# Six places for block rows, keys beside the gather, and output turns inside the last head

## The chip, the cores and the metric

The kernel runs on one core of a Trainium2 chip. A core has five engines that run their own instruction streams and meet at semaphores: PE (TensorE, matrix products and transposes), DVE (VectorE), ACT (ScalarE), POOL (GpSimd) and SP (SyncE, which here only issues DMAs). The metric is device time in microseconds of one execution, lower is better. About 0.2% (5 us) is what a measurement of this kernel can tell from no change.

## The reference

Four gated layers work on x, 2 batches of 1024 tokens with 256 channels, that is 2048 rows or 16 tiles of 128 tokens. All is fp32. Each layer adds an attention part and a feed-forward part to x, both times a tanh gate. The change touches the first three of these eight parts:

```
x = x + tanh(g_xattn[0]) * joint_attention(layernorm(x), context)   # 16 heads of 16; keys of x and of 154 context rows
x = x + tanh(g_ffn[0])   * one_expert(layernorm(x))                 # argmax of 8 experts, gelu, 256 -> 256 -> 256
x = x + tanh(g_xattn[1]) * cross_attention(layernorm(x), context)   # 16 heads of 64; keys and values of the context only
```

In the expert part each token goes through the one expert of eight that its gate ranks highest. In the cross-attention part keys and values are products of the context and of weights; neither depends on x. The queries come from a second layer norm of x with gain and shift.

## The kernel before

Products are made in three passes: each fp32 operand is split into an upper part (rounded to the PE's fp32r form by ACT) and a rest (made by DVE or POOL by a subtraction), and three matmuls add upper by upper, rest by upper and upper by rest. The helper `rest` is line 210, `three` is line 1640, `products` is line 198. The parts of the program follow one another in blocks; at the end of a block all engines meet, and `net.reclaim()` between the stages also clears semaphores.

**Joint attention** (`joint_attention`) runs 32 turns, one for each head of each batch. In a turn PE makes transposed scores for ten key tiles (line 2923), ACT takes exponentials of them (line 2986, two of 128x512 for each key tile), and PE multiplies them with the values (line 2933). Beside it DVE finds row maxima for a head that comes later; in the last turn none is left to find. A turned output is copied by ACT into `o_raw` (lines 2968 and 2976). The first batch's output is normalised by POOL during a later head. Then an output block follows: DVE normalises the second batch (lines 3157 and 3162), PE turns the 16 tiles (line 3100), ACT and DVE split them (lines 3132 and 210), PE multiplies them with `wo`, and DVE adds the products to x (line 3148) and takes row statistics for the next layer norm (lines 95 and 98).

**One expert** (`one_expert`) ranks the experts, gives each token a slot so that every block of 256 slots has one expert, and scatters the normalised rows to `slots_x` in HBM. The loop runs over 15 blocks. For block i, SP loads 256 rows (line 537) into one of NX = 3 places, PE turns them (line 560), ACT and DVE split them (lines 643 and 210), PE makes the hidden layer (`up(i)`, 12 matmuls of 256 columns), ACT applies gelu (line 667), DVE splits it (lines 205 and 210), PE makes the output (`down_mm(i)`, again 12), DVE copies it (line 723) and SP stores it to `slots_y` (line 549). The weights of block i+2 are copied by ACT (line 636) after `down_mm(i-1)`, and their rest is made by POOL (line 210). PE's order is `up(i+1)`, turn of block i+3, `down_mm(i)`. SP's order is load of block i+3, wait for the copied output of block i, store of block i. After the loop POOL waits for the stores and fetches the rows of each token back by 16 indirect DMAs (line 696); DVE adds them to x in four groups and takes statistics (lines 779, 95, 98).

**Cross attention** (`cross_attention`) first runs the layer norm with gain and shift into `xT`, then a block that makes keys and values (ACT splits upper parts, DVE and POOL make rests, PE multiplies; DVE copies values), and then the main block, whose first product needs the split of the first group of rows (`xg`).

Of the kernel before, what the change touches and what calls it, by code (L numbers as in the profile page):

```python
# [19 lines left out]
F32R = mybir.dt.float32r  # L20
ALU = mybir.AluOpType
# [3 lines left out]
P = 128  # L25
# [5 lines left out]
G = 4  # L31
# [5 lines left out]
BLOCK = 256  # L37
NB0 = (NTOK + 8 * (BLOCK - 1)) // BLOCK
# [447 lines left out]
def one_expert(net, xT, xn, x, w, const, scale, slots_x, slots_y, cleared, fetch):  # L486
# [8 lines left out]
    NX, NW, NH, NY = 3, 3, 3, 3  # L495
# [3 lines left out]
    with ExitStack() as ctx:  # L499
# [9 lines left out]
        place, slot, slots = sb("place", [P, T, E]), sb("slot", [P, T]), sb("slots", [P, T], mybir.dt.uint32)  # L509
# [4 lines left out]
        yg = xn  # L514
# [10 lines left out]
        gathered = [sem(f"gathered{g}") for g in range(G)]  # L525
        x_in = [sem(f"x_in{k}") for k in range(NX)]
        stored = [sem(f"stored{k}") for k in range(NY)]
        order = [(n % G) * GT + n // G for n in range(T)]
# [4 lines left out]
        def _(sp):  # L533
# [11 lines left out]
            for i in range(NB):  # L545
                if i + NX < NB:
                    load(i + NX)
                sp.wait_ge(y_taken, i + 1)
                sp.dma_start(rows(slots_y, i), yb[:, i % NY].rearrange("p (h d) -> p h d", h=H))\
                    .then_inc(stored[i % NY], 16)  # L550

        @block.tensor
        def _(pe):
# [10 lines left out]
            def up(i):  # L564
# [4 lines left out]
                for u in range(2):  # L569
                    for c in range(C):  # L570
                        ins = products(pe, net.ps[:, GATE + i % 2, u * BLOCK:(u + 1) * BLOCK],
                                       lambda a: w_parts[a][:, i % NW, 512 * u + c * P:512 * u + (c + 1) * P],
                                       lambda a: x_parts[a][:, i % NX, c * BLOCK:(c + 1) * BLOCK],
# [55 lines left out]
        def _(act):  # L629
# [9 lines left out]
            def take_x(i):  # L639
                act.wait_ge(turned, i + 1)  # L640
                if i >= NX:
                    act.wait_ge(up_done, i - NX + 1)
                act.copy(x_parts[0][:, i % NX, :].bitcast(F32R), net.ps[:, XB[i % len(XB)], :]).then_inc(x_upper, 1)
# [29 lines left out]
            net.rows.root_table(act)  # L673

        @block.gpsimd
        def _(pool):
# [3 lines left out]
            for n, t in enumerate(order):  # L680
# [11 lines left out]
            for k in range(NY):  # L692
                pool.wait_ge(stored[k], 16 * len(range(k, NB, NY)))
            for n in sorted(range(T), key=lambda n: order[n]):
                t = order[n]
                pool.indirect_dma_start(yg[:, t, :], None, slots_y, bass.IndirectOffsetOnAxis(slots[:, n:n + 1], 0))\
                    .then_inc(gathered[t // GT], 16)

        @block.vector
        def _(v):  # L700
# [6 lines left out]
            def rest_x(i):  # L707
                v.wait_ge(x_upper, i + 1)
                rest(v, x_parts[1][:, i % NX, :], net.ps[:, XB[i % len(XB)], :], x_parts[0][:, i % NX, :])\
# [64 lines left out]
            v.wait_ge(init_taken, 2 * G)  # L774
            for g in range(G):
                v.wait_ge(gathered[g], 16 * GT)
                for t in range(g * GT, (g + 1) * GT, 2):
                    xk, yk = (ap[:, t:t + 2, :].rearrange("p t d -> p (t d)") for ap in (x, yg))
                    step(v.scalar_tensor_tensor(xk, yk, scale, xk, ALU.mult, ALU.add))
                step.settle()  # L780
                net.rows.take(v, step, x, range(g * GT, (g + 1) * GT))
# [863 lines left out]
def cross_attention(net, x, factor, w):  # L1645
# [5 lines left out]
    with ExitStack() as outer:  # L1651
# [10 lines left out]
        with ExitStack() as ctx:  # L1662
            layer_norm(net, x, xT, again=True, gain=w("gain"), shift=w("shift"), after=w)
# [7 lines left out]
            wq_upper, wo_upper, cleared, x_upper = sem("wq_upper"), sem("wo_upper"), sem("cleared"), sem("x_upper")  # L1671
# [31 lines left out]
            def _(act):  # L1703
                act.copy(cx[0][:].bitcast(F32R), net.ctxT).then_inc(ctx_upper, 1)
# [6 lines left out]
                act.copy(wq[0][:].bitcast(F32R), w("wq")).then_inc(wq_upper, 1)  # L1711
# [3 lines left out]
                act.copy(wo[0][:].bitcast(F32R), w("wo")).then_inc(wo_upper, 1)  # L1715

            @block.gpsimd
            def _(pool):
                for part in ct:
                    ins = pool.memset(part[:], 0.0)  # L1720
                ins.then_inc(cleared, 1)
# [1856 lines left out]
```

## Time and profile before

| | |
|---|---|
| median of 3 runs | 2550.1 us (2546.55 to 2551.69) |
| the profiled execution | 2544.47 us, of which the span is 2541.5 us |
| mean granted PE clock | 0.901 of full |
| busy: PE, DVE, ACT, POOL | 2058.8, 1769.8, 1328.3, 1049.7 us |

The span runs from the first to the last instruction. Busy time is a sum over the whole span, over stages with different limits. The three places of the change lie between 488 us and 745 us of the span: the last head's turn and the output block (488 to 533), the expert loop (577 to 674), the gather (674 to 703), the layer norm (704 to 714), the keys and values (714 to 739), and the first products of the main block (from 740).

### The profile page before, as it was taken

Reading aid. Unit: us, or ns where it says so; the run is one execution under the profiler, and the core shown is the slowest. Engines: PE = TensorE matmul, PEld = TensorE weight load, DVE = VectorE, ACT = ScalarE, POOL = GpSimd, SP = SyncE. Lnnn points to the kernel's source line nnn. Section 1 sums busy time; section 2 is a strip of 40 time slices with the busy share of each in tenths; the row PEclk is TensorE's granted clock in tenths of the full one; section 3 lists DMA queues with packets and bytes.
Section 4 is the critical chain, followed back from the end, with each engine's and each line's share of the span. In section 5 each row is a group of like instructions: output and inputs, shape, how many; then the busy total and the mean of one; then the engine's idle time right before and its main releaser. Section 6 shows DMA issues by size and latency. Waiting matters only on the chain. (4 is left out here: it accounts for less than half of the span.)

```text
span 2541.5 us, 41197 instructions
## 1 busy us (share of the span) xinstructions
PE 2058.8 (81%) x14707; PEld 1493.9 (59%) x14744; DVE 1769.8 (70%) x3781; ACT 1328.3 (52%) x3055; POOL 1049.7 (41%) x1062
## 2 busy tenths in 40 slices
PE   6899999955479998699998978976998886985254
PEld 5344444345366665588887667765877765764122
DVE  6899999654465555577776676666657676568896
ACT  4588888823255553333333246464435565323797
POOL 1333333023444442255553655552636462422554
PEclk9899999978789998799999898988998988997586
DMA  4244444152200000300001000002000000001000
GB/s 108 32 54 54 50 54 50 19 228 81 83 1 1 1 1 1 129 1 1 1 1 63 23 1 1 1 1 93 1 1 1 1 1 38 1 4 55 0 1 33
DMA packets 27719, 80.79 MB, mean 32 GB/s; under 512 B 6016, under 2 KB 18048, under 8 KB 25856
## 3 DMA queue, kind: packets, MB, share of 16 engines
q0 software_dynamic: 9600, 22.38, 6.8%
q1 hardware_dynamic: 17920, 55.80, 6.4%
q8 instruction: 120, 1.97, 0.3%
q14 instruction: 79, 0.65, 0.1%
HBM read 45.07 MB, written 12.06 MB: 22 GB/s over the span
## 5 line engine op out<-in xcount | busy, mean ns | idle before, releaser
L2986 ACT ACTIVATE probs<-psum 128x512 f32<-128x512 f32 (+1 forms) x640 | 343.9, 601 | 91.3 <-PE psum L2923 75.9
L3025 DVE TENSOR_REDUCE max_parts<-psum 128x1 f32<-128x512 f32 x512 | 320.0, 685 | 26.9 <-PE psum L2871 21.2
L198 PE MATMUL psum<-x_upper,weights_upper 128*128 128x512 f32 (+2 forms) x556 | 221.5, 398 | 26.0 <-POOL weights_rest L210 12.9
L210 POOL TENSOR_TENSOR weights_rest<-L1f,weights_upper 128x256 fp32r<-128x256 f32 x216 | 178.8, 855 | 148.8 <-ACT weights_upper L340 148.8
L2923 PE MATMUL psum<-q_stack,k_stack 50*128 50x512 f32 (+1 forms) x640 | 235.9, 453 | 0.3 <-ACT probs L2986 0.3
L198 PE MATMUL psum<-x_rest,weights_upper 128*128 128x512 f32 (+2 forms) x556 | 218.4, 393 | 0.0
L198 PE MATMUL psum<-x_upper,weights_rest 128*128 128x512 f32 (+2 forms) x556 | 217.0, 390 | 0.0
L2871 PE MATMUL psum<-k_stack,q_stack 48*128 48x512 f32 x512 | 192.8, 465 | 12.8 <-ACT probs L2986 7.7
L2933 PE MATMUL psum<-probs,v_tok 128*17 128x256 f32 x2560 | 195.3, 387 | 0.2 <-ACT probs L2986 0.2
L198 PE MATMUL psum<-weights_upper,hidden_upper 128*128 128x256 f32 (+1 forms) x572 | 180.3, 315 | 5.4 <-DVE hidden_rest L210 2.7
L2516 POOL TENSOR_TENSOR probs<-probs,row_sum 128x1024 f32<-128x1024 f32 x64 | 121.2, 1896 | 138.6 <-DVE row_sum L2535 138.6
L210 POOL TENSOR_TENSOR weights_rest<-L2f,weights_upper 128x256 fp32r<-128x256 f32 (+1 forms) x144 | 104.5, 754 | 163.4 <-ACT weights_upper L340 163.4
L198 PE MATMUL psum<-weights_upper,hidden_rest 128*128 128x256 f32 (+1 forms) x572 | 165.1, 289 | 0.0
L198 PE MATMUL psum<-weights_rest,hidden_upper 128*128 128x256 f32 (+1 forms) x572 | 165.0, 289 | 0.0
L2871 PEld LDWEIGHTS psum<-k_stack,q_stack 48*128 48x128 f32 x512 | 80.0, 189 | 125.0 <-DVE max_parts L3025 69.2
L2484 ACT ACTIVATE probs<-probs,row_least 128x256 f32<-128x256 f32 x256 | 127.0, 498 | 40.6 <-DVE row_least L2529 40.6
L2643 POOL DMA_DIRECT2D q_stack<-q_parts x56 | 30.5, 544 | 264.4 <-PE psum L2923 264.4
L210 DVE TENSOR_TENSOR hidden_rest<-hidden,hidden_upper 128x512 fp32r<-128x512 f32 (+1 forms) x143 | 132.8, 929 | 4.9
L198 PEld LDWEIGHTS psum<-x_upper,weights_upper 128*128 128x128 f32 (+1 forms) x556 | 107.0, 193 | 49.5 <-issue 22.1
L1927 ACT ACTIVATE L1x<-psum,row_least 128x154 f32<-128x154 f32 x256 | 95.6, 400 | 76.3 <-DVE row_least L1981 76.3
L1963 POOL TENSOR_TENSOR L1x<-L1x,row_sum 128x512 f32<-128x512 f32 x64 | 67.8, 1059 | 157.7 <-DVE row_sum L1986 157.3
L2381 POOL TENSOR_TENSOR cos_part<-cos_part,sin_part 128x1024 f32<-128x1024 f32 x32 | 76.5, 2389 | 115.6 <-DVE sin_part L2348 115.6
(508 smaller groups left out, 6061.0 us busy)
## 6 DMA issues: line engine op xcount, KB each, us to landing
k_stack<-k_parts POOLq DMA_DIRECT2D x56, 147.2 KB, 3.8
L1f<-in_L1f SPq DMA_DIRECT2D x1, 6016.0 KB, 22.4
L2f<-in_L2f SPq DMA_DIRECT2D x2, 2268.0 KB, 8.6
L1x<-in_L1x SPq DMA_DIRECT2D x1, 4226.0 KB, 14.6
k_stack<-k_parts POOLq DMA_DIRECT2D x56, 73.6 KB, 4.1
L0f<-in_L0f SPq DMA_DIRECT2D x1, 4096.0 KB, 13.7
L2a<-in_L2a SPq DMA_DIRECT2D x2, 2048.0 KB, 14.7
slots_x<-zeros SPq DMA_DIRECT2D x1, 3840.0 KB, 12.8
```

The costliest lines, as they stand in the source:

```text
L198: ins = pe.matmul(out, lhsT(a).bitcast(F32R), rhs(b).bitcast(F32R), start=start and n == 0, stop=stop and n == len(PASSES) - 1, skip_group ...
L210: return engine.tensor_tensor(dst.bitcast(F32R), src, up_part, ALU.subtract)
L1927: ins = act.activation(ex[:, n % NE, h, :], net.ps[:, SLOT + 2 * s + e, a * SC:(a + 1) * SC], ACT.Exp, bias=mn[:, s, e, a:a + 1], scale=-1 ...
L1963: pool.tensor_tensor(main, ex[:, n % NE, :, 0:P], spread(sm[:, n % NE, :], P), ALU.mult)
L2381: pool.tensor_tensor(cp, cp, s_part[:, t % NSP].rearrange("p a n -> p (a n)"), ALU.add).then_inc(added, 1)
L2484: ins = act.activation(pb[:, n % NPB, h, :], pb[:, n % NPB, h, :], ACT.Exp, bias=mn[:, n % NPB, h:h + 1], scale=-1.0, accum_out=sm[:, n % ...
L2516: pool.tensor_tensor(pb[:, n % NPB], pb[:, n % NPB], spread(sm[:, n % NPB, :], 2 * P), ALU.mult)\
L2871: ins = pe.matmul(out, qs[s][r, a * P:(a + 1) * P].bitcast(F32R), ks[s][r, k * 512:(k + 1) * 512].bitcast(F32R), start=True, stop=True)
L2923: pe.matmul(net.ps[0:m, ST + n % NS, :], ks[s][r, k * P:k * P + m].bitcast(F32R), qs[s][r, :].bitcast(F32R), start=True, stop=True).then_i ...
L2933: ins = pe.matmul(net.ps[32 * j:32 * j + HD + 1, PVB, 0:256], vt[:, b, k, h, :], pb[:, n % NPB, j * 256:(j + 1) * 256], start=k == 0, stop ...
L2986: act.activation(pb[0:m, n % NPB, (1 - e) * 512:(2 - e) * 512], net.ps[0:m, ST + (2 * n + e) % NS, :], ACT.Exp, scale=HD ** -0.5)\
L3025: ins = v.tensor_reduce(mx3[:, u % 2, a + 4 * e, k:k + 1], src, AX.X, ALU.max)
```

## The change

It has three parts.

First, the rows of a block get six places in SBUF (`NX = 6`) where they had three; the split rows keep three (`NP = 3`). SP issues six loads at the start, and in the loop the load of block i+6 stands where that of block i+3 stood.

Second, the gather of the expert part moves into the keys block of cross attention, and the layer norm moves behind that block. The gathered rows go into the memory of `xT`. What POOL did there goes elsewhere: tails of the context are copied by ACT, `ct` and `vz` are cleared by DVE, the second half of `wv` and all of `wo` get their rest from DVE. DVE adds the gathered rows group by group after each pair of value items. The split of the first row group moves to the start of the main block, upper by ACT and rest by DVE, and PE waits for it. The table load for the square root moves from the end of the expert loop to the end of ACT's queue in the keys block.

Third, six of the eight output turns of joint attention (four tiles each) are made in the last head's turn, together with their splits and that of `wo`, in memory of `k_parts`. The two that are left need the last eight heads of the second batch.

```diff
-    NX, NW, NH, NY = 3, 3, 3, 3
+    NX, NP, NW, NH, NY = 6, 3, 3, 3, 3
...
-        x_parts, w_parts = two("x", [P, NX, C * BLOCK]), two("weights", [P, NW, 4 * BLOCK])
+        x_parts, w_parts = two("x", [P, NP, C * BLOCK]), two("weights", [P, NW, 4 * BLOCK])
...
@@ one_expert, sync @@
+            for k in range(NY):
+                sp.wait_ge(stored[k], 16 * len(range(k, NB, NY)))
...
@@ one_expert, end of the gpsimd queue @@
-            for k in range(NY):
-                pool.wait_ge(stored[k], 16 * len(range(k, NB, NY)))
-            for n in sorted(range(T), key=lambda n: order[n]):
-                t = order[n]
-                pool.indirect_dma_start(yg[:, t, :], None, slots_y, bass.IndirectOffsetOnAxis(slots[:, n:n + 1], 0))\
-                    .then_inc(gathered[t // GT], 16)
...
@@ cross_attention, keys block, scalar @@
+                act.wait_ge(tails_cleared, 1)
+                act.wait_ge(ctx_upper, 1)
+                tails(ct[0], cx[0])
+                act.wait_ge(ctx_ready, 1)
+                tails(ct[1], cx[1]).then_inc(tails_ready, 1)
...
                 act.copy(wo[0][:].bitcast(F32R), w("wo")).then_inc(wo_upper, 1)
+                act.copy(wq[0][:].bitcast(F32R), w("wq")).then_inc(wq_upper, 1)
+                net.rows.root_table(act)
...
@@ keys block, gpsimd @@
+                for n in sorted(range(T), key=lambda n: SLOT_TILE[n]):
+                    t = SLOT_TILE[n]
+                    pool.indirect_dma_start(yg[:, t, :], None, slots_y, bass.IndirectOffsetOnAxis(slots[:, n:n + 1], 0))\
+                        .then_inc(gathered[t // GT], 16)
                 pool.wait_ge(wq_upper, 1)
                 rest(pool, wq[1][:], w("wq"), wq[0][:])
-                pool.wait_ge(wo_upper, 1)
-                rest(pool, wo[1][:], w("wo"), wo[0][:])
+                pool.tensor_scalar(gbo[:], w("bo"), factor, None, ALU.mult)
...
@@ keys block, vector @@
+                for n in range(len(v_items)):
+                    value(n)
+                    if n == 1:
+                        v.wait_ge(wo_upper, 1)
+                        rest(v, wo[1][:], w("wo"), wo[0][:])
+                    if n % 2:
+                        add(n // 2)
...
+        layer_norm(net, x, xT, again=True, gain=w("gain"), shift=w("shift"))
...
@@ main block: scalar, vector, tensor @@
+                act.copy(xg[0][:, 0].bitcast(F32R), whole_x(0)).then_inc(first_upper, 1)
+                v.wait_ge(first_upper, 1)
+                rest(v, xg[1][:, 0], whole_x(0), xg[0][:, 0]).then_inc(first_ready, 1)
+                pe.wait_ge(first_ready, 1)
...
@@ joint_attention @@
+            turns = [(0, 0), (0, 1), (1, 0), (1, 1), (2, 0), (3, 0)]
+            turn_at = {0: [0], 1: [1], 2: [2], 3: [3], 4: [4, 5]}
...
+                        if u == NU - 1:
+                            for i in turn_at[k]:
+                                turn_o(i)
...
+                        if u == NU - 1 and k == 0:
+                            act.copy(wo[0][:].bitcast(F32R), w_out("wo")).then_inc(wo_upper, 1)
+                        if u == NU - 1 and k % 2 == 0 and k > 0:
+                            for i in turn_at[k // 2 - 1]:
+                                upper_o(i)
...
+                for i in turn_at[STEPS - 1]:
+                    upper_o(i)
                 copy_out(NU - 1)
                 take_out(NU - 1)
...
@@ output block, tensor @@
+                for g in range(LATE):
+                    project(g)
+                for g in range(LATE, G):
+                    pe.wait_ge(normed, g - LATE + 1)
+                    for j in range(GT):
+                        t = g * GT + j
+                        ins = pe.transpose(net.ps[:, TB + g - LATE, j * P:(j + 1) * P],
+                                           qp[0][:, 1, t // QT, t % QT * P:(t % QT + 1) * P], net.ident[:])
+                    ins.then_inc(turned, 1)
+                for g in range(LATE, G):
+                    project(g)
```

ACT's queue at the last head, before. `probs` are the exponentials, `o_heads` and `o_raw` a head's finished output, `oT_upper` the upper parts of the turned outputs.

```order
L2986 ACTIVATE probs<-psum 128x512 x6
L2976 COPY o_raw<-psum 128x4x17 x2
L2986 ACTIVATE probs<-psum 128x512 x8
L2986 ACTIVATE probs<-psum 26x512 x2
L2968 COPY o_heads<-psum 128x256
L2976 COPY o_raw<-psum 128x4x17 x2
L2797 UNCONDITIONAL_BRANCH
L3126 UNCONDITIONAL_BRANCH
L3128 CAST wo_upper<-L0o 128x512
L3132 CAST oT_upper<-psum 128x512 x8
```

The same end of ACT's queue after the change. `k_parts` is the memory in which the split turns now stand.

```order
L3018 CAST k_parts<-psum 128x512
L3032 ACTIVATE probs<-psum 128x512 x4
L3018 CAST k_parts<-psum 128x512
L3032 ACTIVATE probs<-psum 128x512 x2
L3032 ACTIVATE probs<-psum 26x512 x2
L3018 CAST k_parts<-psum 128x512 x2
L3004 COPY o_heads<-psum 128x256
L3012 COPY o_raw<-psum 128x4x17 x2
L2811 UNCONDITIONAL_BRANCH
L3181 UNCONDITIONAL_BRANCH
L3186 CAST k_parts<-psum 128x512 x2
```

Six of the eight casts of turned outputs moved from the output block to between the exponentials, two of them to just before the last head's copy.

POOL's queue from the gather on, before. `xn` and, after the change, `xT` take the gathered rows; the `ISA` row is the clearing of semaphores between stages.

```order
L696 DMA xn<-slots_y,slots 128x256 x16
L499 UNCONDITIONAL_BRANCH
L79 ISA x2
L1717 UNCONDITIONAL_BRANCH
L1720 MEMSET context_tails_upper 128x512
L1720 MEMSET context_tails_rest 128x512
L1726 CAST context_tails_upper<-context_upper 128x8x26 x2
L1726 CAST context_tails_rest<-context_rest 128x8x26 x2
L1730 MEMSET tail_values 128x2048
L210 TENSOR_TENSOR wv_rest<-L1x,wv_upper 128x2x512
L1734 TENSOR_SCALAR gated_bias<-L1x,cross_factor 128x256
L210 TENSOR_TENSOR wq_rest<-L1x,wq_upper 128x2048
```

POOL's queue at the same place after.

```order
L500 UNCONDITIONAL_BRANCH
L80 ISA x3
L1717 UNCONDITIONAL_BRANCH
L1721 DMA xT<-slots_y,slots 128x256 x16
L211 TENSOR_TENSOR wq_rest<-L1x,wq_upper 128x2048
L1725 TENSOR_SCALAR gated_bias<-L1x,cross_factor 128x256
```

The 16 gathers stand inside the keys block, and all that POOL computed there but one rest and the bias is gone from its queue.

DVE's queue in the keys block after the change (the adds of groups 2 and 3 follow in the same way).

```order
L211 TENSOR_TENSOR wv_rest<-L1x,wv_upper 128x2x512 x2
L1766 MEMSET tail_values 128x2048
L211 TENSOR_TENSOR keys_rest<-psum,keys_upper 128x308 x8
L1736 COPY values<-psum 128x512 x2
L211 TENSOR_TENSOR wo_rest<-L1x,wo_upper 128x2048
L1749 SCALAR_TENSOR_TENSOR x_tok<-xT,tanh_gates,x_tok 128x512 x2
L96 BN_STATS row_stats<-x_tok 128x6 x4
L99 BN_AGGR mean_var<-row_stats 128x2 x4
L1741 COPY tail_values<-psum 32x2x64 x8
L1749 SCALAR_TENSOR_TENSOR x_tok<-xT,tanh_gates,x_tok 128x512 x2
```

The adds and statistics, which stood alone after the loop, now stand between the copies of values.

## Rows read from the trace of the kernel before

**Rows 1.** Busy time by stretch: us, PE, PEld, DVE, ACT, POOL busy; clock, DMA, GB/s.

```profile
488.00:506.00 18.00, 17.51 (x169) 6.36 (x167) 0.56 (x2) 16.37 (x36) 0.00 (x0) 1.00 0.01 1
577.00:674.00 97.00, 62.24 (x420) 58.75 (x420) 46.61 (x60) 37.39 (x61) 29.69 (x28) 0.88 0.25 79
```

**Rows 2.** Waits in the expert loop, 578 to 674: us in total, times, longest.

```profile
PE psum L560 <- DMA block_x<-slots_x: 45.5, 12, 17.5
```

**Rows 3.** Timeline of SP's queue: start us, us, queue, line, out<-in.

```profile
591.44 0.36 SPq L549 DMA_DIRECT2D slots_y<-block_y  x1
591.84 0.47 SPq L537 DMA_DIRECT2D block_x<-slots_x  x1
...
664.76 9.56 SPq L549 DMA_DIRECT2D slots_y<-block_y  x4
```

**Rows 4.** Timeline of PE, first waiting turn of the loop.

```profile
594.72 0.66 PE L560 MATMUL psum<-const,block_x 128*128 128x128 f32 x4 [3.29 <-DMA block_x<-slots_x]
```

**Rows 5.** Timeline of the loop's end, where no rows are left to load.

```profile
663.73 0.28 PE L198 MATMUL psum<-weights_upper,hidden_rest 128*128 128x256 f32 x1
663.85 0.28 PE L198 MATMUL psum<-x_upper,weights_upper 128*128 128x256 f32 x1
...
664.14 1.05 ACT L636 CAST weights_upper<-L0f 128x1024 fp32r x1 [0.94 <-PE psum L198]
...
665.38 2.15 POOL L210 TENSOR_TENSOR weights_rest<-L0f,weights_upper 128x512 fp32r<-128x512 f32 x2 [3.83 <-ACT weights_upper L636]
...
667.62 0.36 PE L198 MATMUL psum<-x_upper,weights_upper 128*128 128x256 f32 x1 [0.74 <-issue]
```

**Rows 6.** Timeline of the gather: POOL's DMAs and DVE's last adds.

```profile
676.91 1.00 POOL L696 DMA_INDIRECT xn<-slots_y,slots  x1 [9.39 <-DMA slots_y<-block_y]
684.53 1.24 POOL L696 DMA_INDIRECT xn<-slots_y,slots  x1 [0.30 <-issue]
696.66 0.96 POOL L696 DMA_INDIRECT xn<-slots_y,slots  x1 [0.30 <-issue]
...
699.42 1.42 DVE L779 SCALAR_TENSOR_TENSOR x_tok<-xn,tanh_gates,x_tok 128x512 f32<-128x512 f32 x2 [2.04 <-DMA xn<-slots_y,slots]
```

**Rows 7.** Timeline of layer norm, keys block and the main block's first product.

```profile
703.92 0.18 DVE L141 TENSOR_SCALAR var_eps<-mean_var 128x16 f32<-128x16 f32 x1 [1.23 <-PEq L80]
714.09 0.70 ACT L1704 CAST context_upper<-const 128x616 fp32r<-128x616 f32 x1 [0.27 <-PEq L113]
718.35 1.37 DVE L210 TENSOR_TENSOR wv_rest<-L1x,wv_upper 128x1024 fp32r<-128x1024 f32 x1
725.41 4.63 POOL L210 TENSOR_TENSOR wq_rest<-L1x,wq_upper 128x2048 fp32r<-128x2048 f32 x1
727.47 3.65 DVE L210 TENSOR_TENSOR x_group_rest<-xT,x_group_upper 128x1024 fp32r<-128x1024 f32 x1
740.34 0.50 PE L1640 MATMUL psum<-x_group_upper,wq_upper 128*128 128x512 f32 x1 [2.73 <-POOL L1x L1955]
```

**Rows 8.** Keys block: PE's clock at start, DVE over three stretches without x_group.

```profile
717.00:719.00 2.00, 1.72 (x7) 1.75 (x8) 2.00 (x3) 2.00 (x3) 2.00 (x3) 0.50 0.00 0
sum 18.70, DVE 15.06; mean DVE 5.02
```

**Rows 9.** Timeline of the last head's turn and the output block.

```profile
488.32 7.68 ACT L2986 ACTIVATE probs<-psum 128x512 f32<-128x512 f32 x14
506.35 0.37 ACT L2968 COPY o_heads<-psum 128x256 f32<-128x256 f32 x1 [0.74 <-PE psum L2933]
507.94 0.62 ACT L3128 CAST wo_upper<-L0o 128x512 fp32r<-128x512 f32 x1 [0.29 <-PEq L2797]
508.59 0.69 DVE L210 TENSOR_TENSOR wo_rest<-L0o,wo_upper 128x512 fp32r<-128x512 f32 x1 [19.46 <-ACT wo_upper L3128]
514.02 0.44 PE L1640 MATMUL psum<-wo_upper,oT_upper 128*128 128x256 f32 x1 [4.13 <-DVE oT_rest L210]
532.13 0.72 DVE L95 BATCH_NORM_STATS2 row_stats<-x_tok 128x6 f32<-128x256 f32 x2
```

More of the change, by code:

```diff
@@ L37 @@
 BLOCK = 256
+SLOT_TILE = [(n % G) * GT + n // G for n in range(T)]
 NB0 = (NTOK + 8 * (BLOCK - 1)) // BLOCK
@@ L1703, in _, with tails @@
             def _(act):
+                def tails(part, src):
+                    for c in range(C):
+                        for b in range(B):
+                            ins = act.copy(part[:, c, b, :, 0:TAIL].bitcast(F32R),
+                                           src[:, c, b * SC + P:(b + 1) * SC].unsqueeze(1).broadcast_to([P, 4, TAIL]))
+                    return ins
+                act.wait_ge(w.landed, 16)
                 act.copy(cx[0][:].bitcast(F32R), net.ctxT).then_inc(ctx_upper, 1)
@@ L1757, in _, with value @@
-                v.wait_ge(cleared, 2)
-                for n, (b, tail, half) in enumerate(v_items):
+                step = Steps(v, vec)
+                def value(n):
+                    b, tail, half = v_items[n]
                     v.wait_ge(v_made, n + 1)
@@ L2832, in joint_attention @@
                             ring.append(("out", u - 1))
+                        if m == 0 and u == NU - 1:
+                            ring += [("turn", i) for i in turn_at[k]]
                         if m == 1 and k == 2 and u + 1 < NU:
@@ L2977, in take_out, with upper_o @@
                     ins.then_inc(out_taken, 1)
+                def upper_o(i):
+                    g, c = turns[i]
+                    act.wait_ge(made, place["turn", i] + 1)
+                    act.copy(oT[0][:, c, g * GN:(g + 1) * GN].bitcast(F32R), bank(("turn", i))).then_inc(o_upper, 1)
                 for u in range(NU):
@@ L3164, in _, with add @@
[L3164 to L3170 removed]
+                step = Steps(v, vec)
+                def add(k):
+                    v.wait_ge(projected, k + 1)
+                    xk = x[:, 2 * k:2 * k + 2, :].rearrange("p t d -> p (t d)")
+                    v.scalar_tensor_tensor(xk, net.ps[:, YB + k % 4, :], tg, xk, ALU.mult, ALU.add)\
+                        .then_inc(y_taken, 1)
@@ new lines, in rows_of @@
+                def rows_of(k):
+                    v.wait_ge(y_taken, k + 1)
+                    net.rows.take(v, step, x, range(2 * k, 2 * k + 2))
+                v.reciprocal(rd[:], o_raw[:, QT:T, HC:H, HD]).then_inc(inverted, 1)
+                v.wait_ge(inverted, 1)
+                for g in range(G - LATE):
+                    at = slice(g * GT, (g + 1) * GT)
+                    v.tensor_tensor(normal(1, 1)[:, at], o_raw[:, QT + g * GT:QT + (g + 1) * GT, HC:H, 0:HD],
+                                    spread(rd[:, at], HD), ALU.mult).then_inc(normed, 1)
@@ new lines, in _ @@
+                add(0)
+                add(1)
+                for k in range(G - LATE):
+                    g = LATE + k
+                    v.wait_ge(o_upper, k + 1)
+                    rest(v, oT[1][:, 1, g * GN:(g + 1) * GN], net.ps[:, TB + k, :],
+                         oT[0][:, 1, g * GN:(g + 1) * GN]).then_inc(o_ready, 1)
+                for k in range(2, 2 * G):
+                    add(k)
+                    rows_of(k - 2)
+                for k in range(2 * G - 2, 2 * G):
+                    rows_of(k)
```

198 lines of the change are left out of this document (81 added, 117 removed).

## The prediction

> **What bounds the kernel now.** I read the busy time by stretch first, then the waits of the expert loop, then the timelines of SP, PE, ACT, POOL and DVE at the three places. The chain that ended last is no help: it covers only the last part of the program. All three places stand before it in one row of stages, so time saved at one of them goes straight to the end, as long as the stages behind it are not changed.
>
> The expert loop is bound by waiting, not by an engine: in 97 us PE is busy 62 us and DVE 47 us, at a mean granted clock of 0.88 [rows 1]. PE waited 45.5 us in 12 waits for block rows; the first, 17.5 us, is before the loop, and the other 11 are 28.0 us, 2.5 us each [rows 2]. The reader should see why: SP issues the load for block i+3 right behind the store of block i-1 (591.44 and 591.84), and PE wants it in the same round; it gets it at 594.72, 2.9 us after the issue [rows 3, 4]. So each round holds copy of the output, store issue, load, turn and `down_mm` in a chain. The twelfth store is issued 73.3 us behind the first, 6.67 us for each of 11 blocks [rows 3].
>
> Between loop and keys POOL issues 16 gathers one after another, 676.91 to 697.6, and nobody else has work [rows 6]. Then come the layer norm (703.92 to 713.8), the keys block and at 740.34 the main block's first product [rows 7].
>
> In the last head ACT makes exponentials back to back (0.55 us each), and PE is busy 17.5 of 18 us at the full clock, so neither has much room; DVE stands idle 19.5 us [rows 1, 9]. In the output block DVE is what ends it: from 508.59 to about 533.1 [rows 9].
>
> **The change, part by part: six places.** The load that PE wants in a round is now issued three rounds earlier. Three rounds are over 10 us, the load takes 2.9 us [rows 3, 4], and DMA is busy a quarter of the loop [rows 1]; so the 28 us go. What is late next is the weights chain or PE. PE's work in a round is 24 matmuls, one every 0.12 us at the full clock (663.73 to 663.85), and four transposes, about 0.5 us: 3.4 us [rows 4, 5]. The weights chain: `down_mm(i-1)` ends at about 664.0, ACT copies from 664.14, POOL makes the rest from 665.38 to 667.53, PE starts `up(i+2)` at 667.62 [rows 5]; that is 3.65 us, beginning when `down_mm(i-1)` ends, and PE fills it with `up(i+1)`, a turn and `down_mm(i)`, 3.4 us. So a round takes 3.65 us if both run at their best. DVE has 46.6 / 15 = 3.1 us of work in a round [rows 1] and just fits. The clock stands at half after the waits of today and should stay at its full level without them. The gain is 11 x (6.67 - 3.65) = 33.2 us. Bounds: 11 x 2.5 = 28 us if only the waits go [rows 2], and 37 us if POOL's part is hidden as well and each round is PE's 3.4 us plus the slow clock saved. I take 33.2. The three more loads at the start queue behind the first three, which alone are wanted there; cost nothing.
>
> **Gather beside the keys.** Measured from the stores' landing (676.9) to the first product of the main block (740.34) the stretch is 63.4 us. After: semaphores and barrier 1.2 us [rows 7]; keys block; layer norm with its two borders 10.2 us (703.92 to 714.09) [rows 7]; split of the first group: ACT casts 128x1024 in 1.05 us [rows 5], DVE's rest 1.37 us [rows 7], with hand-overs 2.7 us. The keys block is now bound by DVE. Its old work without the x group is 15.1 us [rows 8]. Added: second half of `wv` 1.4 and rest of `wo`, twice the size, 2.7 [rows 7]; three clears with 3072 elements a row, at most 4.1 us at the same rate, I take 2.7; four groups of adds and statistics, each 3.3 us (699.42 to 702.69, which is 1.23 before 703.92), 13.1 [rows 6, 7]. Sum 35.0. It waits for ACT's first cast (0.7) and some 2 us for keys from a cold PE, and loses about 1.5 us beside POOL's rest of `wq`: 39 us. POOL needs 20.7 + 4.6 + 0.9 = 26 us, hidden [rows 6, 7]. ACT's tails and its new last copies stand beside DVE's values and cost nothing. Total 1.2 + 39 + 10.2 + 2.7 = 53.1, a gain of 10.3 us. Against it: PE starts the main block at 740 at the full clock since the values came just before; after a layer norm it starts at half, as the keys block does now (0.50 at 717 to 719) [rows 8]. Twelve matmuls of 512 columns and the first scores at half speed cost about 2.5 us. I take 7.8. Bounds: DVE as low as 34 us gives 13; DVE slowed by half wherever POOL reads (1024 elements took 3.65 us in place of 1.37 beside `wq`) for five such operations, 11 us, gives -3 [rows 7].
>
> **Turns in the last head.** ACT gets one cast of `wo` (0.62) and four of turned outputs (0.6 each) between its exponentials, 3.0 us; two more stand where ACT waited 0.74 us for PE, so about 0.5 us of these is new [rows 9]. PE gets 24 transposes, 2.9 us, beside ACT's. Since both are nearly full I take 4.0 us; bounds 3.0 and, if the two don't overlap, 6.4 us. DVE's share (six rests, `wo`, one half of the normalising) falls into its 19.5 us of idle time [rows 9]. The output block loses on DVE six rests, the rest of `wo` and two of four normalising products, nine operations of about 0.65 us: 5.9 us. PE starts to multiply at once instead of at 514.02 [rows 9], but the order makes DVE wait for the two last turns behind eight tiles' products (about 5.7 us), so that its block is about 19.6 us long where it was 25.2. Gain 5.6 - 4.0 = 1.6 us, from -0.8 to +2.6.
>
> **Sum.** 33.2 + 7.8 + 1.6 = 42.6 us. The profiled execution took 2544.5 us, so its counterpart would take 2501.9; it stands 5.6 us below the median of the runs shown, and the median would go from 2550.1 to 2507.5 us.
>
> **A rule of the skill.** Among the gathers of today the one that ran beside DVE's adds took 1.24 us where the others took 0.96 [rows 6]. The Trainium skill ("SBUF — State Buffer", section "SBUF: two separate sides") says that a DMA issued by GpSimd needs a port that DVE locks while it copies fp32 from SBUF to SBUF, and that such a DMA took 3100 ns where it takes 620 alone. By that difference, an estimate from that page, 16 gathers would be 40 us longer, POOL would end the keys block at 66 us, and the time would be about 2535. The row shows a much smaller price, and DVE has no SBUF-to-SBUF copy in the new keys block, so the trace and the same page's condition both speak for little.
>
> **Rivals.** (a) DVE becomes the bound of the loop. POOL's part of the weights takes 2.15 us [rows 5], so it now stands beside DVE in most of each round of 3.65 us, and beside POOL a DVE operation of 1.37 us has taken 3.65 [rows 7]. If that adds 1.3 us to DVE's 3.1 us a round [rows 1], a round takes 4.4 us and the loop gains 11 x (6.67 - 4.4) = 25 us: 2516 us. Against it: DVE's 3.1 us are a mean that has such overlaps in it already. (b) The loads stay late because they queue with the stores: no gain in the loop, 2541 us. Against it: DMA is busy 0.25 [rows 1]. (c) Slower than before: the gathers starve beside DVE. If each of the 16 waited out a DVE operation like the 3.65 us one [rows 7], it would take 4.9 us, POOL 79 + 5.6 = 84 us, 45 us more than the 39 of the keys block, and the time would be 2553 us. It decides from about 4.6 us a gather on; today's worst is 1.24 [rows 6].
>
> **How the numbers follow.** Forecast 2500 to 2516 us: 0.60. More gain, under 2500: 0.08. (a), 2516 to 2523: 0.20. Between that and 2540, several parts short: 0.04. (b) 0.05, (c) 0.03. The range 2496 to 2524 holds the forecast and (a) and leaves out less than 2 in 10. About 0.2%, 5 us, is what a measurement can tell: faster 0.95, same 0.02, slower 0.03.
>
> **What would show it.** In the loop PE's waits for `block_x` should vanish but for the first, stores come some 3.7 us apart, and the clock be near 1.0. The gathers should stay near 1 us, the keys block end with DVE's last statistics about 39 us after its start. The last head should be 4 us longer and the output block 5 to 6 us shorter. I am wrong if stores stay over 4.5 us apart, if a gather takes over 2 us, or if DVE is idle for long in the keys block.

## The result and the profile after

| | before | after |
|---|---|---|
| median of 4 runs each | 2550.89 us (2546.55 to 2555.43) | 2507.49 us (2504.96 to 2513.76) |
| profiled execution, span | 2544.47, 2541.5 us | 2507.33, 2505.4 us |
| mean granted PE clock | 0.901 | 0.903 |

The ratio is 0.9833, with a 95% interval of 0.9808 to 0.9858: 43 us faster by the medians. The two profiled spans differ by 36.1 us. Read by stages, with after's time less before's:

| stage, from and to | before | after | difference | forecast |
|---|---|---|---|---|
| start to first head's `o_heads` copy | 103.3 | 108.3 | +4.9 | none |
| last head, between its two last `o_raw` copies | 19.38 | 22.62 | +3.2 | +4.0 |
| last `o_raw` copy to `var_eps` of the layer norm | 28.17 | 22.62 | -5.6 | -5.6 |
| layer norm to first store of the loop | 55.96 | 57.36 | +1.4 | none |
| loop, first store to last `block_y` copy | 82.50 | 47.56 | -34.9 | -33.2 |
| last `block_y` copy to main block's first product | 66.40 | 62.32 | -4.1 | -10.3 |
| main block, to the next `var_eps` | 292.35 | 294.07 | +1.7 | +2.5 |
| the rest of the program | 1508.8 | 1505.8 | -3.0 | none |

The stretch between the first two rows, 384.6 and 384.8 us, is left out. The first and the last row are not the change's doing. Both executions run the same code up to 100 us, but the clock rose later in this one. These are the windows of 80 to 100 us, first of before, then of after; the number behind POOL is the granted clock.

```profile
80.00:100.00 20.00, 18.17 (x121) 8.21 (x121) 18.11 (x35) 9.84 (x19) 0.00 (x0) 0.64 0.01 2
```

```profile
80.00:100.00 20.00, 18.17 (x91) 8.13 (x91) 15.99 (x31) 7.61 (x14) 0.00 (x0) 0.50 0.01 2
```

The same copy stands at 102.9 to 103.7 us in some executions of the kernels below and at 108.2 to 109.8 us in others. So one profile is 5 us longer than another for nothing, and stages have to be compared instead of spans.

**The loop.** SP's queue, to compare with [rows 3], and the longest waits of 570 to 680 us with the one that [rows 2] shows:

```profile
595.62 0.36 SPq L547 DMA_DIRECT2D slots_y<-block_y  x1
...
606.55 0.36 SPq L547 DMA_DIRECT2D slots_y<-block_y  x1
606.95 0.47 SPq L535 DMA_DIRECT2D block_x<-slots_x  x1
610.39 0.36 SPq L547 DMA_DIRECT2D slots_y<-block_y  x1
610.80 0.47 SPq L535 DMA_DIRECT2D block_x<-slots_x  x1
613.70 0.36 SPq L547 DMA_DIRECT2D slots_y<-block_y  x1
...
624.70 14.07 SPq L547 DMA_DIRECT2D slots_y<-block_y  x5
```

```profile
POOL weights_rest L211 <- ACT weights_upper L636: 26.2, 13, 9.0
...
PE psum L560 <- DMA block_x<-slots_x: 17.0, 2, 16.8
```

Only the wait ahead of the loop is left. The ninth store is issued 29.1 us behind the first, 3.64 us a round, and most rounds take 3.31 and 3.84 us in turn. The window of these rounds has the clock at full:

```profile
595.00:625.00 30.00, 28.78 (x239) 28.09 (x238) 23.97 (x33) 19.57 (x34) 17.74 (x18) 1.00 0.46 141
```

PE is busy 28.8 of 30 us. In every second round it waits for POOL's rest of the weights, here 613.17 + 2.14 = 615.31, and starts `up` at 615.41 when its last product had begun at 614.83:

```profile
613.17 2.14 POOL L211 TENSOR_TENSOR weights_rest<-L0f,weights_upper 128x512 fp32r<-128x512 f32 x2 [1.71 <-ACT weights_upper L636]
```

```profile
614.83 0.28 PE L199 MATMUL psum<-weights_upper,hidden_rest 128*128 128x256 f32 x1
615.41 0.36 PE L199 MATMUL psum<-x_upper,weights_upper 128*128 128x256 f32 x1 [0.31 <-issue]
```

**The keys block** runs from 646.88 (ACT's first cast) to 693.47 (`var_eps`), 46.6 us where 39 were forecast. DVE's queue shows both reasons; to compare with [rows 6, 7, 8]:

```profile
662.15 0.48 DVE L211 TENSOR_TENSOR keys_rest<-psum,keys_upper 128x308 fp32r<-128x308 f32 x1 [2.36 <-issue]
663.23 0.69 DVE L1736 COPY values<-psum 128x512 f32<-128x512 f32 x1 [0.60 <-PE psum L1625]
666.70 0.69 DVE L1736 COPY values<-psum 128x512 f32<-128x512 f32 x1 [2.78 <-PE psum L1625]
667.31 2.28 DVE L211 TENSOR_TENSOR wo_rest<-L1x,wo_upper 128x2048 fp32r<-128x2048 f32 x1
669.50 6.11 DVE L1749 SCALAR_TENSOR_TENSOR x_tok<-xT,tanh_gates,x_tok 128x512 f32<-128x512 f32 x2
...
679.79 1.42 DVE L1749 SCALAR_TENSOR_TENSOR x_tok<-xT,tanh_gates,x_tok 128x512 f32<-128x512 f32 x2
```

```profile
651.00 1.95 POOL L1721 DMA_INDIRECT xT<-slots_y,slots  x1 [0.30 <-issue]
653.25 0.95 POOL L1721 DMA_INDIRECT xT<-slots_y,slots  x1 [0.30 <-issue]
...
670.42 4.51 POOL L211 TENSOR_TENSOR wq_rest<-L1x,wq_upper 128x2048 fp32r<-128x2048 f32 x1
```

The first pair of adds took 6.1 us where the next took 1.42, and it ends at 675.6, 0.7 us after POOL's rest of `wq`, which is one add's own time: the first add was through, the second waited. And DVE's second copy of values waits 2.8 us for a product whose last matmul of PE had started at 661.9:

```profile
661.89 0.40 PE L1625 MATMUL psum<-wv_upper,context_rest 128*128 128x512 f32 x1
```

ACT's last copy of keys is late in the same way; the last matmul of its product had started at 659.21. The row names a scatter as what ended the wait, but what the program has ACT wait for there is PE's product.

```profile
661.70 0.42 ACT L1712 CAST keys_upper<-psum 128x308 fp32r<-128x308 f32 x1 [2.42 <-DMA slots_x<-xn,slots]
```

**The last head** is as thought. ACT's casts of turned outputs stand between exponentials, and DVE waits 3.1 us for the two late ones in the output block [rows 9]:

```profile
513.75 1.04 ACT L3018 CAST k_parts<-psum 128x512 fp32r<-128x512 f32 x2
514.69 0.36 ACT L3004 COPY o_heads<-psum 128x256 f32<-128x256 f32 x1
```

```profile
523.28 1.29 DVE L211 TENSOR_TENSOR k_parts<-psum,k_parts 128x512 fp32r<-128x512 f32 x2 [3.13 <-ACT k_parts L3186]
```

PE begins the output block at once, and its second half follows these two rests:

```profile
516.29 5.90 PE L1625 MATMUL psum<-k_parts 128*128 128x256 f32 x48 [0.69 <-PEq L2811]
524.03 5.91 PE L1625 MATMUL psum<-k_parts 128*128 128x256 f32 x48 [0.96 <-DVE k_parts L211]
```

**The main block** waits for the split of the first group, 12.0 us after the start of the layer norm, where 12.9 were given (10.2 and 2.7):

```profile
705.50 0.50 PE L1625 MATMUL psum<-x_group_upper,wq_upper 128*128 128x512 f32 x1 [4.37 <-DVE x_group_rest L211]
```

### The profile page after: what moved, and what is told of

Same layout as the page of the kernel before. It is cut to its first block and busy times, and to the rows that moved or that the text cites. A ratio compares the mean times of both kernels' runs of the same rounds, so it can differ in the third digit from the quotient of the medians.

```text
span 2505.4 us, 41257 instructions
## 1 busy us (share of the span) xinstructions
PE 2059.0 (82%) x14744; PEld 1489.0 (59%) x14744; DVE 1768.8 (71%) x3786; ACT 1328.6 (53%) x3064; POOL 1036.9 (41%) x1053
## 5 line engine op out<-in xcount | busy, mean ns | idle before, releaser
L199 PE MATMUL psum<-x_upper,weights_upper 128*128 128x512 f32 (+2 forms) x556 | 219.8, 395 | 28.2 <-POOL weights_rest L211 12.9
```

The lines of the kernel that those rows point to most:

```text
L199: ins = pe.matmul(out, lhsT(a).bitcast(F32R), rhs(b).bitcast(F32R), start=start and n == 0, stop=stop and n == len(PASSES) - 1, skip_group ...
```

## The experiments

"Loop", "keys block" and the like are the stages of the table, and ratios are against the kernel before, with 95% intervals. The changed kernel's is 0.9833 [0.9808, 0.9858].

### Each part alone

`e1_places`: the kernel before with the first part.

```diff
-    NX, NW, NH, NY = 3, 3, 3, 3
+    NX, NP, NW, NH, NY = 6, 3, 3, 3, 3
```

> Kernel before with the first part alone: six places for block rows, three for their split parts. Theory (the loads' lateness was the loop's bound, and each part stands by itself): from the first store to the last block_y copy 47 to 48 us where before had 82.5, and the whole is 33 to 36 us faster than before; keys block and last head as in before. Rival (the loop got faster in the changed kernel because something else of the change helped it, such as the stores' waits or the moved gather): the loop keeps 60 us or more and the gain stays under 25 us.

Measured: the loop took 47.59 us, and 66.50 us went from its last copy to the main block. The ratio is 0.9865 [0.983, 0.990], which is 34 us of 2550. The loads are the whole of the loop's gain, and it needs no other part.

`e2_keys`: the second part alone (`NX = 3`, joint attention as before).

> Kernel before with the second part alone: gather and adds beside keys and values, layer norm behind them. Theory (two thirds of the forecast gain is lost in stalls of the keys block itself): last block_y copy to the main block's first product about 62 us where before had 66.4, keys block about 46 us, its stalls at the same places (DVE's first add over 5 us beside POOL's wq_rest, two gaps of over 2 us on ACT and DVE), the whole 1 to 4 us faster. Rival (the keys block was slow only because the loop's stores and the shorter loop stand just before it): keys block about 39 us, stretch 55 us, the whole 8 us or more faster.

Measured: 58.1 us went from the last copy to the main block where before has 66.4, and the keys block took 42.5 us. The ratio is 0.9965 [0.9949, 0.9981], which is 9 us. It lies between the two theories. An add of 6.42 us beside POOL is there, so that stall belongs to the part. The late copies are not there, against the theory: they came with something else of the change.

`e3_turns`: the third part alone.

> Kernel before with the third part alone: six turns of the joint output in the last head. Theory: last head 3.2 us longer, output block 5.5 us shorter, and 1 us of that given back in the waits behind it; the whole 1 to 2.5 us faster, which the timing alone can't tell from none. Rival (the later rise of the clock at 80 to 140 us of the span in the changed kernel comes from the changed joint attention code): this kernel too has copies of the first head's output 5 us later than before, and is 2 us or more slower than before.

Measured: from the first head's copy to `var_eps` 430.0 us, in the kernel before 432.1 and in the changed one 430.0. So the part gives 2.1 us there. The rival falls, since the first copy is at 102.9 us. The ratio is 0.9975 [0.9964, 0.9986], 3.6 to 9.2 us, more than the expected 1 to 2.5; its own profile does not show where the surplus would come from (its span is 1.7 us longer than before's), and that stays open.

By their ratios the three parts alone give 34, 9 and 6 us, together 50, and the changed kernel 43. The intervals are too wide to tell the two from each other.

### How far ahead the loads run

`e4_four`: the changed kernel with `NX = 4`.

> Changed kernel with four places for block rows in place of six. Theory (a load takes 2.9 us, a round 3.6 us, so a load issued one round earlier is just in time): stores 3.6 to 3.8 us apart, time within 3 us of the changed kernel. Rival (the load meets the store's traffic and DMA is busy half of the loop, so one round ahead is not enough): PE waits for block_x again, stores 4 us apart or more, and the whole is 4 us or more above the changed kernel.

Measured: ratio 0.9827 [0.9806, 0.9848], not to be told from the changed kernel. The loop took 49.6 us, 2 more: PE waited again for `block_x`, 2.1 us in four times. Both theories have a part of it. The keys block had no late copies and took 42.5 us.

`e12_four_ahead`: six places, but each load issued four blocks ahead.

```diff
-            for i in range(NX):
+            for i in range(4):
                 load(i)
             for i in range(NB):
-                if i + NX < NB:
-                    load(i + NX)
+                if i + 4 < NB:
+                    load(i + 4)
```

> Changed kernel, still with six places, but SP issues each load four blocks ahead and not six. Two questions. Loop: theory (only how early a load is issued matters, not how many places there are): 49 to 50 us from first store to last copy as with four places, two us more than the changed kernel. Keys block: copies of PE's last key and first values came 2 to 7 us late in the five profiles with five or six places and in none of the five with three or four. Theory A (it hangs on the places, that is on memory or on the number of instructions): late here too, keys block about 46.5 us. Theory B (it hangs on how far ahead the loads run): 42.5 us.

Measured: the loop took 49.5 us as in `e4` and the keys block 42.5 us, and the ratio is 0.9819 [0.980, 0.9838]. So the earliness of the issue counts in the loop and not the number of places. The late copies are gone as well, with memory and semaphores as in the changed kernel. So theory A falls, and theory B got its number; but that the distance of the loads brings the late copies about isn't shown by it, as the last section says.

`e9_spare_sems`: `e4` with two unused semaphores, which give the keys block the same semaphore numbers as in the changed kernel.

```diff
-        x_in = [sem(f"x_in{k}") for k in range(NX)]
+        x_in = [sem(f"x_in{k}") for k in range(NX + 2)]
```

> Kernel of e4 (four places for block rows) plus two semaphores that are allocated in the expert part and never used; they shift the numbers of the keys block's semaphores to those of the changed kernel. In the profiles of the changed kernel, e5, e6, e7 and e8 copies of PE's last key and first values began 2 to 7 us after PE's product had ended, with nothing else to wait for; in e2 and e4 they followed within 0.6 us. Theory A (the lateness comes with the numbers of the semaphores): here it is back, ACT's last keys copy waits about 2.4 us and the keys block takes 45 us or more. Theory B (it comes with five or six row places as such, or by chance of an execution): the keys block takes 42.4 us as in e4.

Measured: the keys block took 42.5 us, and nothing was late. Theory A falls: these semaphore numbers alone don't bring the lateness.

### What bounds the keys block

`e5_wq_dve`: DVE makes the rest of `wq`.

```diff
 @@ gpsimd @@
-                pool.wait_ge(wq_upper, 1)
-                rest(pool, wq[1][:], w("wq"), wq[0][:])
 @@ vector @@
+                    if n == 3:
+                        v.wait_ge(wq_upper, 1)
+                        rest(v, wq[1][:], w("wq"), wq[0][:])
```

> Changed kernel with one edit: the rest of wq is made by DVE (2.3 us, as wo's rest took there) behind its copy of the fourth value item, not by POOL behind the gathers. Theory (DVE's add took 6.1 to 6.4 us in place of 1.4 because POOL read wq and its upper part from SBUF at the same time): no add over 1.5 us is left but perhaps one beside the bias product; keys block 40 us where e2 and e4 had 42.4 and the changed kernel's profile 46.4; 2 to 3 us faster than the changed kernel's like. Rival (the long add waits for its gathered rows or for DVE's port beside POOL's indirect DMAs): an add of 4 us or more stays and the keys block is 44 us or longer.

Measured: every pair of adds takes 1.41 or 1.42 us. First the second pair of `e4` beside POOL, then the same pair of `e5`:

```profile
668.02 6.41 DVE L1749 SCALAR_TENSOR_TENSOR x_tok<-xT,tanh_gates,x_tok 128x512 f32<-128x512 f32 x2
```

```profile
668.44 4.55 POOL L211 TENSOR_TENSOR wq_rest<-L1x,wq_upper 128x2048 fp32r<-128x2048 f32 x1
```

```profile
675.89 1.41 DVE L1747 SCALAR_TENSOR_TENSOR x_tok<-xT,tanh_gates,x_tok 128x512 f32<-128x512 f32 x2
```

In `e4` the pair ends at 674.43, which is 1.44 us after POOL's end at 672.99. It waited out POOL's operation and then ran at its normal rate. The first add is on record 0.42 us before POOL's operation and was held up all the same (in `e2` it is 0.44 us), so its loss, 5.0 us, is more than the whole of POOL's 4.55. `e5`'s keys block took 46.8 us all the same, against the expected 40: the copies were late here by more, 4.8 us for the second value, which fed DVE's sum. The time shows 0.9815 [0.9796, 0.9834], which is no sure gain. The edit's worth is seen in `e10`, where nothing is late: 40.1 us in place of 42.5.

`e6_act_values` and `e7_both`: ACT copies values and tail values; DVE adds the groups one behind the other. `e7` has `e5`'s edit as well, its rest of `wq` between `add(1)` and `add(2)`. The definition of `value`, which moves from DVE's part to ACT's, and DVE's old loop are left out here.

```diff
 @@ scalar, behind the copies of keys @@
+                act.wait_ge(cleared, 1)
+                for n in range(4):
+                    value(n)
                 act.copy(wo[0][:].bitcast(F32R), w("wo")).then_inc(wo_upper, 1)
                 act.copy(wq[0][:].bitcast(F32R), w("wq")).then_inc(wq_upper, 1)
+                for n in range(4, 8):
+                    value(n)
 @@ vector @@
+                add(0)
+                v.wait_ge(wo_upper, 1)
+                rest(v, wo[1][:], w("wo"), wo[0][:])
+                add(1)
...
+                add(2)
+                add(3)
```

> Changed kernel with the copies of values and tail values moved from DVE to ACT, and DVE adding the four groups one behind the other with the rest of wo behind the first. Theory (DVE's sum is what ends the keys block; ACT is idle there for 24 us): DVE loses 7.4 us, PE no longer waits for it, and the end is set by the sixteenth gather, 24 us after the start, its landing, the last add beside POOL's wq_rest (6.2 us) and its statistics: keys block 32 to 36 us, 7 to 10 us faster than the changed kernel. Rival (POOL's gathers are slowed where DVE runs without PSUM operands in between): gathers of over 2 us become common, the sixteenth ends 30 us or more after the start, keys block 39 us or more.

> The two edits of e5 and e6 together. Theory: keys block ends with the last gathered group's add and statistics, 3.3 us behind the landing of the sixteenth gather (about 26 us after the start): 30 to 32 us, 3 us less than e6, 11 to 13 us faster than the changed kernel before the cold clock. Rival (as for e6): 36 us or more, no faster than e6.

Measured: keys blocks of 44.4 and 43.2 us, ratios 0.9827 [0.9803, 0.9852] and 0.9805 [0.9786, 0.9825]. Both theories missed. In `e7` no gather after the fourth took over 1.5 us, so the gathers were not slow; it was ACT that now waited for PE's values, 1.8, 4.4 and 2.3 us, and DVE waited behind it. Both rows are of `e7`:

```profile
669.22 0.58 ACT L1702 COPY values<-psum 128x512 f32<-128x512 f32 x1 [4.36 <-DMA slots_x<-xn,slots]
```

```profile
676.17 2.29 DVE L211 TENSOR_TENSOR wo_rest<-L1x,wo_upper 128x2048 fp32r<-128x2048 f32 x1 [9.99 <-ACT wo_upper L1730]
```

The lateness follows the consumer of PE's product, from DVE in `e5` to ACT in `e7`, so it is between PE and whoever waits. The trace's record of semaphore updates says on which side: PE's signal for the second value product of `e7` is on record at 669.20, 6.9 us after the product's last matmul had started, and ACT's copy begins at 669.22. In the kernels without late copies the signal stands 0.4 us after that start. So it is the signal that is late, not the engine that waits for it.

### What bounds the loop now, and the sum

`e8_four_weights`: four places for the split weights, five for rows.

```diff
-    NX, NP, NW, NH, NY = 6, 3, 3, 3, 3
+    NX, NP, NW, NH, NY = 5, 3, 4, 3, 3
```

> Changed kernel with four places for the split weights of a block and five for its rows (six and four do not fit). Theory (in every other round PE waits 0.55 us for POOL's rest of the weights, whose upper part ACT may copy only once down_mm(i-1) has freed the place; three rounds in four of PE's own work take 3.30 us): all rounds 3.3 us, first store to last block_y copy 44 to 45 us where the changed kernel had 47.6; 3 us faster. Rival (the long rounds come from gelu, DVE's split of hidden or from DMA traffic): rounds stay at a mean of 3.6 us, no gain.

Measured: the loop took 44.3 us, with seven rounds in a row of 3.30 to 3.33 us, and the ratio is 0.9793 [0.9775, 0.9812]. The keys block had the late copies and took 47.3 us, so the gain is the loop's. PE is the bound, busy 30 of 30 us:

```profile
590.00:620.00 30.00, 30.00 (x257) 30.00 (x255) 22.82 (x36) 20.43 (x37) 18.80 (x18) 1.00 0.52 159
```

`e10_mix`: four places for rows and for weights, with `e5`'s edit. `e11_mix_act`: the same with `e7`'s.

> Changed kernel with four places for rows, four for the split weights and the rest of wq made by DVE. Theory (the parts add up): loop 44 to 46 us, keys block 40 us if no signal of PE is late, 44 if it is; 2495 to 2499 us. Rival (four row places are too few for rounds of 3.3 us): PE waits for block_x 5 us or more in the loop and nothing is gained on e8's 2498.

> As e10, with the copies of values and tail values made by ACT (the edit of e6). In e6 and e7 it gained no more than 3 us, since ACT was late by 2 to 7 us at the first values and made wo's upper part, which DVE waited 10 us for, only behind them. Theory (without the late signals): keys block 32 to 35 us, time 2488 to 2493 us. Rival (the signals are late here too): keys block 43 us as in e7, time as e10's.

Measured: `e10` has a keys block of 40.1 us as expected, but a loop of 47.5 us, and a ratio of 0.9816 [0.9796, 0.9835]. At 3.3 us a round a load four blocks ahead comes late now and then. The price is what shorter rounds had gained, 3.2 us, though PE's waits for `block_x` sum up to 1.9 us only; neither the theory nor the rival has it so:

```profile
628.77 0.66 PE L560 MATMUL psum<-const,block_x 128*128 128x128 f32 x4 [1.17 <-DMA block_x<-slots_x]
```

`e11` has a keys block of 35.8 us, a loop of 47.2, a median of 2488.4 us and a ratio of 0.9763 [0.9748, 0.9779]. It is the fastest: its interval lies below the changed kernel's, 17.9 us of 2550 by the ratios. Of these the profiles show 11.2 us (10.8 in the keys block, 0.4 in the loop). Its four other executions have a mean granted clock of 0.907 to 0.910 where the changed kernel's four have 0.901 to 0.907, so part of the rest may be the clock's rise and not the edit. Its profiled execution took 2499.8 us, with the late clock rise at the start, and the others 2487.6 to 2493.6. DVE still waits 4.4 us for `wo_upper`, which ACT makes behind four items of values:

```profile
671.01 2.29 DVE L211 TENSOR_TENSOR wo_rest<-L1x,wo_upper 128x2048 fp32r<-128x2048 f32 x1 [4.44 <-ACT wo_upper L1730]
```

`e8`'s five places and `e11`'s keys block were not tried together.

## Why the prediction was right, point by point

- **Loop, 33.2 us: right.** 34.9 us, and 34 in `e1` alone. The step "a round takes 3.65 us" met 3.635 on the mean. The cause given, the weights chain, is half of it: every second round is PE's own 3.31 us. `e8` frees the chain and gets seven in a row to 3.30 to 3.33. The clock at full was right.
- **Rival (a), DVE becomes the bound: wrong.** DVE's work is stretched beside POOL (the cast of `hidden` took 1.35 and 0.8 us in turn, where it takes 0.43 alone, and ended each time 0.3 us after POOL's rest), but PE was busy 28.8 of 30 us.
- **Rival (b), loads late behind stores: no.** A load takes 2.9 us as before. `e4` and `e12` show how near it is: two blocks less ahead cost 2 us.
- **Gather beside keys, 7.8 us: too high.** From last copy to main block only 4.1 us went, less the main block's 1.7. The step that failed is "It ... loses about 1.5 us beside POOL's rest of `wq`": the loss was 4.7 us (6.11 less 1.42), and 5.0 in `e4`. [Rows 7] had it, read wrongly: DVE's 3.65 us began at 727.47 and ended at 731.12, 1.1 us after POOL's 725.41 + 4.63 = 730.04. That is waiting until POOL ends and then running 1.2 us, not running at a third of the rate. The Trainium skill ("SBUF — State Buffer", section "SBUF: two separate sides") says that a DVE operation with two inputs in SBUF and a GpSimd one that reads SBUF block each other for a whole instruction. By that rule the loss is the rest of POOL's 4.6 us. The changed kernel agrees: the second add lost the 4.7 us up to POOL's end. In `e4` the 5.0 us are a little more than the rule gives, since the add is on record as the first to start.
- **Not foreseen: the late copies.** 46.6 less 42.5 is 4.1 us of the changed kernel's keys block. Between its first and last operation DVE stood idle for 7.6 us in the block, which the prediction had named as a sign of its being wrong. Its own work was a little less than forecast: 38.1 us busy less the stall of 4.7 is 33.4, where the sum gave 35.0. Without them (`e2`, `e4`) the stretch is 7.8 to 8.3 us shorter than before's, where the step gave 10.3.
- **Gathers near 1 us, rival (c): right in sum.** 13 of 16 took 0.95 to 1.00 us, the others 1.81, 1.95 and 2.04, and one of `e4` 2.73. The prediction named a gather of over 2 us as a sign against it; the one that was costs nothing, as POOL is not the bound. The slow ones ran beside DVE's rests of weights, which read two operands from SBUF; the argument that DVE has no SBUF-to-SBUF copy there missed these. Of the price that was estimated from the Trainium skill's figures, 2.5 us more a gather ("SBUF — State Buffer", section "SBUF: two separate sides"), the traces show 0.9 to 1.8 us, and for three of 16 gathers.
- **The cold clock of the main block, 2.5 us: right in kind, somewhat high.** In the first 5 us of the block the granted clock was at full before and 0.66 on the mean after; the first row is of before, the second of after, the number behind POOL is the clock:

```profile
740.34:745.34 5.00, 4.14 (x28) 3.15 (x30) 1.38 (x2) 2.48 (x3) 0.00 (x0) 1.00 0.00 0
```

```profile
705.50:710.50 5.00, 5.00 (x18) 3.73 (x18) 0.69 (x1) 0.96 (x2) 0.00 (x0) 0.66 0.00 0
```

  From the block's first matmul to the start of the last one of its fourth query product (`wq_rest` by `x_group_upper`) it is 11.6 us in all three profiles with the old order (before, `e1`, `e3`), 13.2 in the changed kernel, and 13.1 to 14.1 in the eleven with the new order. So the cold start cost 1.6 us here and 1.5 to 2.5 elsewhere. Over the whole block, to the next `var_eps`, it is harder to see: the eleven have 293.8 to 296.4 us, on the mean 294.6, the three 288.5, 292.4 and 295.6, on the mean 292.1.
- **Joint attention, 1.6 us: right.** The last head took 3.2 us more and the output block 5.6 us less, where +4.0 and -5.6 were given.
- **The total.** The median of 2507.5 us is the forecast's. The working by its own measure gave 2501.9 us for the profiled execution, and that took 2507.3. The later rise of the clock took 4.9 us, the stretch of the keys block 6.2 us more than given, and the way from layer norm to loop 1.4 us; the loop gave 1.7 us more than forecast, last head and main block 0.8 us each, the unchanged rest 3.0 us and the time outside the span 1.1 us. That the median met the forecast so nearly is partly luck.

## What to carry to other kernels

Count how many rounds ahead a load is issued, times the length of a round, against its time to landing plus the store it shares the queue with; and count again after each shortening of the round. When work moves beside a POOL operation that reads SBUF, price each two-input SBUF operation of DVE at the whole remaining POOL operation, and give such operations to DVE or keep them apart. Compare stages between fixed points, since a span can be 5 us off from what happens in its first 100 us.

## What the runs showed of the hardware

ACT and DVE began to copy PE's last key product and first values late in the keys block, up to 7.5 us after the last matmul of a product had started, in five profiles: the changed kernel, `e5`, `e6`, `e7` and `e8`. They have the gather beside the keys, and issue loads five or six blocks ahead in the loop before. In the six profiles with the gather there and loads three or four ahead (`e2`, `e4`, `e9` to `e12`) nothing was late, and neither in `e1`, with six ahead and no gather there. `e12` differs from the changed kernel in the distance alone.

The distance is an unlikely cause, though, for the traces of the same five differ from all others before the first load is issued. The 16 scatters ahead of the loop signal 256 landings; the five traces hold 140 to 150 of them, the other nine all 256. In the changed kernel these scatters are issued from 558.0 to 577.3 us, and the first load at 579.8. At 559.9 a signal of PE is missing from the record too, though DVE went on in time. Of the 256 landings of the gathers the five hold 89 to 103, where the others have all again. This is the stretch in which PE's signals come late; in the changed kernel those of the third to the sixth value product then stand within 0.9 us of each other. So the lateness goes with gaps in the record, and whether the recording itself brings it about, or something that these five programs share, stays open.

Whether the executions without a profile have it is open too. The medians of `e5` and `e10`, 2502.3 and 2503.1 us, do not show the 6.7 us between their keys blocks. Those of `e7` and `e11`, 2501.4 and 2488.4 us, differ by more than the 7.4 us between theirs, at the higher clock that `e11` had.

A POOL `TENSOR_TENSOR` that reads SBUF holds up a DVE operation with two SBUF inputs to its end, for up to 5.0 us here, while `keys_rest`, which reads one operand from PSUM, took its usual 0.48 us beside it in the kernel before. A cast with one input in SBUF and its output there is held up as well: in the loop `hidden_upper` took 1.35 us where it takes 0.43 alone, and it ended at 601.29, 0.3 us after POOL's rest of the weights (598.86 to 601.00).
